# A graph network's edge gathers: more groups fetched by SyncE and ScalarE, and columns prepared one chunk further ahead

## The chip, the cores and the metric

The kernel runs on 1 core of one Trainium2 chip. The metric is the device time of one execution, in microseconds. The engines are TensorE (PE; PEld is its weight load), VectorE (DVE), ScalarE (ACT), GpSimd (POOL) and SyncE (SP, which only issues DMAs).

## The reference, cut to what matters

There are 12500 nodes with 96 features and 200000 edges (src, dst), sorted by dst. Four passes over the edges, called rounds 0 to 3 here, follow each other: two mean aggregations and two maxima.

```python
h = relu(layernorm(x))
n1 = segment_sum(h[src], dst) / max(deg, 1)          # round 0
n2 = segment_sum(n1[src], dst) / max(deg, 1)         # round 1
x = x + 0.5 * n1 + 0.5 * n2
h = relu(layernorm(x))
def egnn(X, Wm, We, Wr, b):                          # rounds 2 and 3
    msg = X[src] @ Wm + edge_attr @ We               # edge_attr: 200000 x 32
    agg = segment_max(msg, dst)                      # 0 where a node has no edge
    return agg + X @ Wr + b
out = x + leaky_relu(egnn(leaky_relu(egnn(h, ...1)), ...2))
```

## The kernel before

**Tables and groups.** Each round gathers rows of 96 floats from a table in HBM (`tables[r]`): h, n1, h @ Wm of round 2, and the same of round 3. The edges are cut into batches of 128, one edge a partition, 4 batches (GRP) make a group, and there are 391 groups. The row numbers lie in `src_sb`. A group is gathered by 4 indirect DMAs of GpSimd (line 412), 128 rows each, into one of RING = 8 slots of `rows`; 8 groups are a sweep, and there are 49 sweeps, the last with 7 groups. The place of a group in its sweep is its seat, and its slot has the same number. GpSimd's program is written out, one gather after the other. Before it fills a slot again it waits until TensorE has used the group 8 before (`picked` in rounds 0 and 1, `rows_ps` in rounds 2 and 3).

**Groups aside.** Some groups aren't gathered by GpSimd. In every 12th sweep (SPAN) the group in seat 3 (SEAT) is fetched by SyncE into a buffer of its own, `side`: 99, 195, 291 and 387. For each of 128 partitions SyncE loads 4 row numbers into registers (`numbers`, line 269) and issues 4 DMAs of one row (line 317): 512 DMAs a group. In rounds 0 and 1 (`side_sums`) it does so in one piece, as soon as TensorE has used the group aside before. In rounds 2 and 3 (`load_units`) SyncE also loads, for each unit of 4 groups, flags (768 KB, line 334) and edge features (256 KB, line 336) into one of two buffers, once the unit before the last one that is loaded has been scanned; the rows aside are spread behind the 24 units of a stretch, 5 or 6 partitions behind each.

**What is done with a group.** Rounds 0 and 1: VectorE makes one-hot matrices of a group two ahead (line 824, and in round 0 also line 829 for counting), TensorE multiplies the rows with them (line 614), and VectorE adds the windows to `comp`, the compressed sums by node (`fold`, line 841). In round 0 ScalarE also writes the node number beside each row (`stage_ids`, line 474), up to 8 groups ahead. Rounds 2 and 3: TensorE adds edge features times weights (line 633) and the transposed rows (line 635) in PSUM, VectorE runs a segmented maximum (line 856), TensorE transposes it back (line 646) and picks each segment's end with one-hots (line 657), and ScalarE copies PSUM into `runT` (line 482) and into `comp` (line 491).

**Between the rounds**, and behind the last, the nodes are worked off in 14 chunks of 7 tiles (`nodes` on each engine). For a chunk ScalarE loads 7 starting columns (`windows_of`, line 269), copies 7 blocks of `comp` into `win_f`, which has two buffers (line 531), TensorE transposes them into one place of PSUM (line 695), ScalarE copies that out into `win_c` (line 551), VectorE and GpSimd make one-hots (lines 929 and 426; POOL_HOTS says how many of 7 are GpSimd's), and TensorE spreads the rows to their nodes (line 719). In rounds 0 and 3 this last step comes one chunk later; in rounds 1 and 2 it comes in the same chunk and in the same PSUM as the transposes, so that the next transposes wait until VectorE has read it (line 987 or 995). ScalarE prepares chunk k + 1 right behind chunk k's copy out. The results go to the next table (line 311) or to the output (line 371).

Of the kernel before, what the change touches and what calls it, by code (L numbers as in the profile page):

```python
# [35 lines left out]
P = 128  # L36
# [10 lines left out]
SPAN = 12  # L47
SEAT = 3
# [3 lines left out]
SIDES = (SWEEPS - 1) // SPAN  # L52
SIDE = [((b + 1) * SPAN) * RING + SEAT for b in range(SIDES)]
UNITS = 2 * SPAN
# [17 lines left out]
assert SIDES * SPAN == SWEEPS - 1 and SEAT < UNIT and SIDE[-1] < GROUPS  # L72
# [33 lines left out]
def gnn(nc, x, srcs, cur, prev, nxt, cur_r, prev_r, eat, wm1, we1, wr1, b1, wm2, we2, wr2, b2, out):  # L106
    with ExitStack() as ctx:
# [36 lines left out]
        side = sb("side", [P, GRP, X])  # L144
# [65 lines left out]
        POOL_HOTS = {0: 2, 1: 7, 2: 5, 3: 4}  # L210
# [13 lines left out]
        side_in = {r: [sem(f"side_rows_landed_{r}_half{k}") for k in range(2)] for r in rounds}  # L224
# [33 lines left out]
        def sweeps(engine, body):  # L258

            body(0, RING, 0, False)  # L260
            for b in range(SIDES):
                at = (b + 1) * SPAN
                with engine.Fori(at - SPAN + 1, at) as i:
                    body(i, RING, b, False)
                body(at, RING if at < SWEEPS - 1 else LAST, b, True)

# [10 lines left out]
        def _(sp):  # L277
# [35 lines left out]
            def side_rows(r, b, p):  # L313

                at = bass.ds(b * (SPAN * RING * GRP) + SIDE[0] * GRP, GRP)
                for k, row in enumerate(numbers(sp.engine, src_sb[p:p + 1, at], N - 1)):
                    sp.dma_start(side[p:p + 1, k, 0:D], tables[r][bass.ds(row, 1), :]).then_inc(side_in[r][k % 2], 16)  # L317

            def side_sums(r):

                for s in range(2):
                    sp.wait_ge(tstored[r][s], 16 * (CHUNKS // 2))
                with sp.Fori(0, SIDES) as b:
                    sp.wait_ge(picked[r], b * (SPAN * RING) + (SEAT + 1))
                    for p in range(P):
                        side_rows(r, b, p)

            def load_units(r):
# [12 lines left out]
                for u in range(2):  # L341
                    unit(0, u, UNIT)

                def stretch(b, last):

                    sp.wait_ge(rows_ps[r], b * (SPAN * RING) + (SEAT + 1))
                    for t in range(UNITS):
                        unit(b * SPAN + (1 + t // 2), t % 2, LAST - UNIT if t == UNITS - 1 and last else UNIT)
                        for p in range(t * P // UNITS, (t + 1) * P // UNITS):
                            side_rows(r, b, p)  # L350

                with sp.Fori(0, SIDES - 1) as b:
                    stretch(b, False)
                stretch(SIDES - 1, True)

            side_sums(0)
# [6 lines left out]
            side_sums(1)  # L363
# [17 lines left out]
        def _(pool):  # L381
# [19 lines left out]
            for r in range(ROUNDS):  # L401
# [31 lines left out]
        def _(act):  # L433
# [32 lines left out]
            for r in range(ROUNDS):  # L466

                def stage_ids(i, n, b, aside):
                    for j in range(n):
                        g = i * RING + j  # L470
                        if after(i, 1):
                            act.wait_ge(picked[0], g - (RING - 1))
                        to = side if aside and j == SEAT else rows[:, j]
                        act.copy(to[:, :, D + 1], node1[:, bass.ds(i * (RING * GRP) + j * GRP, GRP)]  # L474
                                 ).then_inc(ids_ready, 1)

# [47 lines left out]
                def windows_of(k, s):  # L524

                    w = X if r == 0 else D
                    starts = numbers(act.engine, node_base[0:1, bass.ds(k * CHUNK, CHUNK)])
# [51 lines left out]
        def _(pe):  # L579
# [10 lines left out]
            for r in range(ROUNDS):  # L590
                def gathered(i, j, b, aside):

                    if aside and j == SEAT:
                        for k in range(2):
                            pe.wait_ge(side_in[r][k], (b + 1) * (P * GRP * 8))
                        return side
                    seen = i - b if j == SEAT else i
# [73 lines left out]
                if r in sums:  # L671
                    pe.wait_ge(prep, PREP_ALL)
                    sweeps(pe, sum_windows)
                else:
                    if r == 2:
                        pe.wait_ge(s_w, 16 * 8)
                    sweeps(pe, max_windows)
# [70 lines left out]
        def _(dve):  # L748
# [64 lines left out]
            step(dve.memset(side[:, :, D], 1.0))  # L813
            assert steps[0] == PREP_ALL

            for r in range(ROUNDS):
# [61 lines left out]
                if r in sums:  # L878
                    hots(0, 0)
                    hots(1, 1)  # L880
# [21 lines left out]
                sweeps(dve, add_windows if r in sums else run_maxima)  # L902
# [134 lines left out]
```

## Time and profile before

| | us |
|---|---|
| median of 3 runs | 8210.22 (8205.53 to 8218.09) |
| the profiled execution | 8212.45 |
| its span | 8210.7 |
| GpSimd busy | 6032.1 (73%) |
| TensorE busy, weight loads | 5197.4, 3879.2 |
| VectorE, ScalarE busy | 3292.4, 1509.8 |
| mean granted TensorE clock | 0.67 of full |

The span is the time from the first to the last instruction. Busy times overlap each other. "issue" in the chain is time in which an engine waited for nothing that the profile shows. The granted clock has two levels here, 0.5 (1.2 GHz) and 1.0 (2.4 GHz).

### The profile page before, as it was taken

What the parts mean: (1) busy time and instruction counts of PE and PEld (TensorE: products, weight loads), DVE (VectorE), ACT (ScalarE), POOL (GpSimd) and SP (SyncE); (2) the same over time, 40 slices, a digit from 0 to 9 for tenths busy, and PEclk for the clock granted to TensorE, in tenths of its full rate; (3) what the DMA queues carried; (4) which work ended last, traced back from release to release, by engine and by line L of the source; (5) the groups of instructions that cost most, each with busy time, mean ns of one, the idle gap of its engine ahead of it and who ended that gap; (6) DMA issues with size and microseconds to landing.
All of it is one profiled execution on the core that took longest, in us unless ns stands there. A gap on an engine that the chain in (4) does not pass through costs nothing.

```text
span 8210.7 us, 127758 instructions
## 1 busy us (share of the span) xinstructions
PE 5197.4 (63%) x25651; PEld 3879.2 (47%) x25651; DVE 3292.4 (40%) x6694; ACT 1509.8 (18%) x5077; POOL 6032.1 (73%) x6461
## 2 busy tenths in 40 slices
PE   3444444445444444444578888888887887878887
PEld 2333333334333333333556655566565555655556
DVE  5444444444433333333433333333343333333334
ACT  2000000001000000000333333323332332333333
POOL 6777777776677777777667777777766777777776
PEclk6555555555555555555687888878888888888887
DMA  3111111111211111111144444444424444444442
GB/s 91 40 40 40 40 41 40 40 40 41 58 40 40 40 40 41 40 41 40 37 96 91 95 93 92 96 91 92 96 61 96 91 97 91 94 94 91 96 92 70
DMA packets 324280, 551.26 MB, mean 67 GB/s; under 512 B 198824, under 2 KB 198824, under 8 KB 299048
## 3 DMA queue, kind: packets, MB, share of 16 engines
q0 software_dynamic: 198144, 304.75, 18.2%
q1 hardware_dynamic: 125188, 242.68, 11.7%
q14 instruction: 353, 2.89, 0.1%
q8 instruction: 47, 0.77, 0.0%
q10 hardware_dynamic: 548, 0.17, 0.0%
HBM read 522.27 MB, written 24.87 MB: 67 GB/s over the span
## 4 chain that ended last, share of the span: by engine, by line
POOL 65%; issue 22%; PE 8%; DMA 3%; ACT 1%; ACTq 1%; DVE 0%; SPq 0%; DVEq 0%; POOLq 0%
POOL rows L412 65%; DMA rows<-table,src_sb 3%; PE ps L635 2%; PE ps L633 2%; PE ps L657 1%; PE ps L719 1%; PE ps L695 1%; ACTq L269 0%; PE ps L646 0%; ACT arena L457 0%; PE ps L732 0%; ACT arena L531 0%; DMA table<-arena 0%; ACT arena L551 0%; SPq L317 0%
## 5 line engine op out<-in xcount | busy, mean ns | idle before, releaser
L412 POOL DMA_INDIRECT rows<-table,src_sb x6192 | 5848.0, 944 | 1975.8 <-issue 1868.0
L614 PE MATMUL ps<-arena,rows 128*98 128x128 f32 (+1 forms) x6192 | 1557.4, 433 | 2154.0 <-DMA rows<-table,src_sb 1286.8
L614 PEld LDWEIGHTS ps<-arena,rows 128*98 128x98 f32 (+1 forms) x6192 | 1296.4, 279 | 2439.4 <-DVE comp L841 2157.6
L856 DVE TENSOR_TENSOR_SCAN arena<-arena,ps 96x512 f32<-96x512 f32 x782 | 997.6, 1276 | 2450.7 <-PE ps L635 2447.9
L841 DVE TENSOR_TENSOR comp<-comp,ps 98x128 f32 (+1 forms) x3128 | 895.7, 286 | 2262.6 <-PE ps L614 1947.4
L633 PE MATMUL ps<-arena,we 32*96 32x512 f32 x1564 | 1033.6, 745 | 721.5 <-DMA rows<-table,src_sb 704.0
L635 PEld LDWEIGHTS ps<-ident,rows 128*96 128x96 f32 x6192 | 865.9, 195 | 754.1 <-issue 754.1
L824 DVE TENSOR_TENSOR arena<-ps,meta 128x512 f32<-128x512 f32 x1564 | 1050.9, 672 | 32.4 <-issue 28.8
L635 PE MATMUL ps<-ident,rows 128*96 128x128 f32 x6192 | 1062.8, 326 | 0.0
L491 ACT COPY comp<-ps 96x128 f32 x3128 | 818.9, 262 | 1088.4 <-PE ps L657 830.5
L657 PE MATMUL ps<-arena 128*96 128x128 f32 x6256 | 968.5, 306 | 1.6 <-ACT arena L482 1.6
L657 PEld LDWEIGHTS ps<-arena 128*96 128x96 f32 x6256 | 865.2, 193 | 2.1 <-ACT arena L482 2.1
L482 ACT COPY arena<-ps 128x384 f32<-128x384 f32 x782 | 373.8, 478 | 1622.7 <-PE ps L646 1620.8
L633 PEld LDWEIGHTS ps<-arena,we 32*96 32x96 f32 x1564 | 218.4, 182 | 865.4 <-DMA rows<-table,src_sb 708.6
L646 PE MATMUL ps<-ident,arena 96*128 96x96 f32 x3128 | 470.4, 282 | 0.3 <-DVE arena L856 0.3
L646 PEld LDWEIGHTS ps<-ident,arena 96*128 96x128 f32 x3128 | 406.6, 168 | 0.8 <-DVE arena L856 0.8
L474 ACT COPY rows<-root 128x4 f32 (+1 forms) x387 | 75.7, 197 | 1799.0 <-PE ps L614 1799.0
L539 ACT COPY rel_c<-node_rel 128x7 f32<-128x7 f32 (+1 forms) x42 | 8.5, 202 | 1943.0 <-DVE comp L841 1943.0
L426 POOL TENSOR_SCALAR arena<-iota,rel_c 128x128 f32<-128x128 f32 x252 | 170.9, 693 | 191.8 <-ACT rel_c L539 107.5
L829 DVE TENSOR_TENSOR arena<-ps,meta 128x392 bf16<-128x392 f32 x391 | 217.4, 556 | 0.0
L620 PE MATMUL ps<-arena,ones_b 128*1 128x392 bf16 x391 | 189.4, 485 | 0.0
L719 PE MATMUL ps<-arena 128*128 128x96 f32 (+1 forms) x784 | 137.7, 348 | 6.2 <-ACT arena L551 4.8
(91 smaller groups left out, 1068.8 us busy)
## 6 DMA issues: line engine op xcount, KB each, us to landing
arena<-flags SPq DMA_DIRECT2D x194, 768.0 KB
side<-table SPq DMA_DIRECT2D x8192, 0.4 KB
rows<-table,src_sb POOLq DMA_INDIRECT x6192, 2.5
arena<-in_eat SPq DMA_DIRECT2D x194, 256.0 KB
table<-arena SPq DMA_DIRECT2D x56, 336.0 KB, 2.7
out<-xs SPq DMA_DIRECT2D x13, 336.0 KB
xs<-in_x SPq DMA_DIRECT2D x6, 672.0 KB, 5.3
arena<-flags SPq DMA_DIRECT2D x2, 576.0 KB
```

Of the source, the lines that this page charges most:

```text
L412: pool.indirect_dma_start(rows[:, g % RING, j, 0:D], None, tables[r][:, :], bass.IndirectOffsetOnAxis(src_sb[:, c:c + 1], 0)).then_inc(lan ...
L482: act.copy(runT[:, slot % SCANS].rearrange("p k d -> p (k d)"), ps[:, RUNT + slot % 2 * BANK:RUNT + slot % 2 * BANK + GRP * D]).then_inc(r ...
L491: act.copy(comp[0:D, bass.ds(at, P)], ps[0:D, WIN + slot % 2 * BANK + j * P:WIN + slot % 2 * BANK + (j + 1) * P]).then_inc(folded[r], 1)
L614: m = pe.matmul(ps[0:w, at + k * P:at + (k + 1) * P], got[:, k, 0:w], hot[:, j % HOTS, k, :], start=True, stop=True)
L633: pe.matmul(ps[0:D, at:at + W], we[D:P, r - 2, :], fe[D:P, u, q * W:(q + 1) * W], start=True, stop=False)
L635: m = pe.matmul(ps[0:D, at + k * P:at + (k + 1) * P], got[:, k, 0:D], ident[:, :], start=False, stop=(k == GRP - 1))
L646: m = pe.transpose(ps[:, at:at + D], run[:, slot % SCANS, k * P:(k + 1) * P], ident[0:D, 0:D])
L657: m = pe.matmul(ps[0:D, at:at + P], runT[:, slot % SCANS, k, :], hot[:, slot % HOTS, k, :], start=True, stop=True)
L719: m = pe.matmul(ps[:, at_spread + j * P:at_spread + j * P + w], spread_c[:, qs, j, :], win_c[:, qs, j, 0:w], start=True, stop=True)
L824: dve.tensor_tensor(hot[:, slot % HOTS], ids.unsqueeze(1).to_broadcast([P, GRP, P]), rel, ALU.is_equal).then_inc(hot_ready[r], 1)
L841: dve.tensor_tensor(win, win, ps[0:w, of:of + P], ALU.add).then_inc(folded[r], 1)
L856: dve.tensor_tensor_scan(run[:, slot % SCANS], fe[0:D, slot // UNIT, q * W:(q + 1) * W], ps[0:D, ROWS + slot % 2 * BANK:ROWS + slot % 2 * ...
```

## The change

- Which groups are aside now depends on the round. Rounds 0 and 1: every 8th sweep, seats 2 and 3, 6 times two groups, SyncE fetching seat 2 and ScalarE seat 3. Rounds 2 and 3: every 9th sweep, seat 0, 5 groups, by SyncE.
- `side` has two buffers, with semaphores for each.
- The node numbers beside the rows in round 0 are written by VectorE, two groups ahead, and not by ScalarE.
- Between the rounds ScalarE copies chunk k + 2 into `win_f` behind chunk k's copy out, where it was chunk k + 1. Chunks 0 and 1 are done at the start; the registers of chunk 0 are loaded ahead of the wait for the last fold.
- In round 0 GpSimd makes 3 of a chunk's 7 one-hots, where it was 2.

```diff
-SPAN = 12
-SEAT = 3
+SPAN = {0: 8, 1: 8, 2: 9, 3: 9}
+SEATS = {0: (2, 3), 1: (2, 3), 2: (0,), 3: (0,)}
-SIDES = (SWEEPS - 1) // SPAN
-SIDE = [((b + 1) * SPAN) * RING + SEAT for b in range(SIDES)]
-UNITS = 2 * SPAN
+SIDES = {r: (SWEEPS - 1) // SPAN[r] for r in SPAN}
+ASIDE = {r: [(b + 1) * SPAN[r] * RING + seat for b in range(SIDES[r]) for seat in SEATS[r]] for r in SPAN}
...
-        POOL_HOTS = {0: 2, 1: 7, 2: 5, 3: 4}
+        POOL_HOTS = {0: 3, 1: 7, 2: 5, 3: 4}
...
+        def side_rows(engine, r, e, b, p):
+
+            at = bass.ds(b * (SPAN[r] * RING * GRP) + (SPAN[r] * RING + SEATS[r][e]) * GRP, GRP)
+            for k, row in enumerate(numbers(engine.engine, src_sb[p:p + 1, at], N - 1)):
+                engine.dma_start(side[p:p + 1, e, k, 0:D], tables[r][bass.ds(row, 1), :]).then_inc(side_in[r, e][k % 2], 16)
+
+        def side_sums(engine, r, e):
+
+            for s in range(2):
+                engine.wait_ge(tstored[r][s], 16 * (CHUNKS // 2))
+            with engine.Fori(0, SIDES[r]) as b:
+                engine.wait_ge(picked[r], b * (SPAN[r] * RING) + (SEATS[r][e] + 1))
+                for p in range(P):
+                    side_rows(engine, r, e, b, p)
...
-                def stretch(b, last):
-
-                    sp.wait_ge(rows_ps[r], b * (SPAN * RING) + (SEAT + 1))
-                    for t in range(UNITS):
-                        unit(b * SPAN + (1 + t // 2), t % 2, LAST - UNIT if t == UNITS - 1 and last else UNIT)
-                        for p in range(t * P // UNITS, (t + 1) * P // UNITS):
-                            side_rows(r, b, p)
...
+                units = 2 * SPAN[r]
+                with sp.Fori(0, SIDES[r]) as b:
+                    sp.wait_ge(rows_ps[r], b * (SPAN[r] * RING) + (SEATS[r][0] + 1))
+                    for t in range(units):
+                        unit(b * SPAN[r] + (1 + t // 2), t % 2, UNIT)
+                        for p in range(t * P // units, (t + 1) * P // units):
+                            side_rows(sp, r, 0, b, p)
+                with sp.Fori(SIDES[r] * SPAN[r] + 1, SWEEPS - 1) as i:
+                    for u in range(2):
+                        unit(i, u, UNIT)
+                unit(SWEEPS - 1, 0, UNIT)
+                unit(SWEEPS - 1, 1, LAST - UNIT)
...
-                    if g in SIDE:
+                    if g in ASIDE[r]:
                         continue
                     if g >= RING:
-                        pool.wait_ge(used, (g - RING if g - RING not in SIDE else g - 2 * RING) + 1)
+                        pool.wait_ge(used, (g - RING if g - RING not in ASIDE[r] else g - 2 * RING) + 1)
...
-                if r == 0:
-                    sweeps(act, stage_ids)
-                elif r in maxima:
-                    sweeps(act, extract)
+                if r in sums:
+                    act.wait_ge(s_src, 16)
+                    side_sums(act, r, 1)
+                else:
+                    sweeps(act, r, extract)
...
-                act.wait_ge(folded[r], COLS)
...
                         if r:
                             stage_rel(0, 0)
-                        windows_of(0, 0)
+                        first = starts_of(0)
+                        act.wait_ge(folded[r], COLS)
+                        windows_of(0, 0, first)
+                        windows_of(1, 1, starts_of(1))
...
-                        windows_of(k + 1, 1 - s)
+                    if not known(k) or k + 2 < CHUNKS:
+                        windows_of(k + 2, s, starts_of(k + 2))
...
+                def stage_ids(g, j, aside):
+
+                    if after(g, RING):
+                        dve.wait_ge(picked[0], g - (RING - 1))
+                    to = side[:, SEATS[0].index(j)] if aside and j in SEATS[0] else rows[:, j]
+                    dve.tensor_copy(to[:, :, D + 1], node1[:, bass.ds(g * GRP, GRP)]).then_inc(ids_ready, 1)
...
                             hots(g + 2, j + 2)
+                            if r == 0:
+                                stage_ids(g + 2, (j + 2) % RING, aside)
```

The helpers `sweeps` and `gathered` take the round and follow SPAN and SEATS of it.

## Rows read from the trace of the kernel before

**Rows 1.** The page: busy time of each engine; the chain that ended last.

```profile
PE 5197.4 (63%) x25651; PEld 3879.2 (47%) x25651; DVE 3292.4 (40%) x6694; ACT 1509.8 (18%) x5077; POOL 6032.1 (73%) x6461
...
POOL 65%; issue 22%; PE 8%; DMA 3%; ACT 1%; ACTq 1%; DVE 0%; SPq 0%; DVEq 0%; POOLq 0%
```

**Rows 2.** Who waited for what: total us, times, longest.

```profile
POOL rows L412 <- issue: 1868.0, 6127, 0.3
...
POOL rows L412 <- PE ps L635: 18.3, 60, 0.3
...
PE ps L633 <- DMA side<-table: 9.8, 4, 4.8
```

**Rows 3.** Line 412, rounds 0 and 2: ns min/median/max, first and last start.

```profile
L412 POOL DMA_INDIRECT rows<-table,src_sb x1548: 940/944/1936, 60.3 to 1995.8; - x194
...
L412 POOL DMA_INDIRECT rows<-table,src_sb x1548: 940/944/1031, 4134.3 to 6065.7; - x194
```

**Rows 4.** SyncE's timeline, first block of rows aside: start, us.

```profile
89.02 293.89 SPq L317 DMA_DIRECT2D side<-table  x512
```

**Rows 5.** Line 438, ScalarE's one-row DMAs at the start: ns min/median/max.

```profile
L438 ACTq DMA_DIRECT2D wcat<-in_b x2: 321/452/583, 2.3 to 4.5; - x2
```

**Rows 6.** Lines 317 and 269, DMA issues and register loads: count, ns min/median/max.

```profile
L317 SPq DMA_DIRECT2D side<-table x8192: 224/227/321, 89.0 to 8109.9; - x200
...
L269 SPq TENSOR_LOAD <-src_sb x2048: 458/471/745, 88.3 to 8107.9; - x187
...
L269 ACTq TENSOR_LOAD <-base x782: 304/309/327, 4160.4 to 8129.8; - x196
```

**Rows 7.** Windows, GpSimd's gathers: stretch, us, busy (count), clock, DMA share.

```profile
90.00:380.00 290.00, 219.25 (x233) 0.50 0.19 41
390.00:560.00 170.00, 128.52 (x137) 0.50 0.19 39
```

**Rows 8.** SyncE's timeline in round 2: a unit's flags, the rows behind it.

```profile
4620.99 0.32 SPq L334 DMA_DIRECT2D arena<-flags  x1
...
4622.56 13.31 SPq L317 DMA_DIRECT2D side<-table  x24
```

**Rows 9.** TensorE's timeline in round 2, two groups one behind the other.

```profile
4630.01 2.02 PE L633 MATMUL ps<-arena,we 32*96 32x512 f32 x2 [6.01 <-DMA rows<-table,src_sb]
...
4636.26 2.02 PE L633 MATMUL ps<-arena,we 32*96 32x512 f32 x2
```

**Rows 10.** VectorE's timeline at the end of round 2, the last scans.

```profile
6076.82 1.27 DVE L856 TENSOR_TENSOR_SCAN arena<-arena,ps 96x512 f32<-96x512 f32 x1 [1.36 <-PE ps L635]
...
6080.10 1.28 DVE L856 TENSOR_TENSOR_SCAN arena<-arena,ps 96x512 f32<-96x512 f32 x1 [1.42 <-PE ps L635]
```

**Rows 11.** Line 531 behind round 0; TensorE's timeline there.

```profile
L531 ACT COPY arena<-comp x98: 292/293/299, 2006.4 to 2072.5; 98x128 f32 x98
...
2053.21 2.46 PE L719 MATMUL ps<-arena 128*128 128x98 f32 x14
2057.42 1.40 PE L695 MATMUL ps<-ident,arena 98*128 98x98 f32 x7 [1.75 <-ACT arena L531]
2058.62 3.19 PE L719 MATMUL ps<-arena 128*128 128x98 f32 x14
```

**Rows 12.** The timeline behind round 1, TensorE's transposes of the second chunk.

```profile
4032.93 1.36 PE L695 MATMUL ps<-ident,arena 96*128 96x96 f32 x7 [1.04 <-DVE arena L987]
```

**Rows 13.** The page: line 474, ids beside the rows.

```profile
L474 ACT COPY rows<-root 128x4 f32 (+1 forms) x387 | 75.7, 197 | 1799.0 <-PE ps L614 1799.0
```

**Rows 14.** Timelines of round 0: gathers and VectorE's work beside them.

```profile
78.78 1.83 POOL L412 DMA_INDIRECT rows<-table,src_sb  x1 [0.30 <-issue]
...
79.52 0.98 DVE L887 CAST meta<-root 128x1564 bf16<-128x1564 f32 x1
...
415.37 0.56 DVE L829 TENSOR_TENSOR arena<-ps,meta 128x392 bf16<-128x392 f32 x1
415.48 0.94 POOL L412 DMA_INDIRECT rows<-table,src_sb  x1 [0.31 <-issue]
```

More of the change, by code:

```diff
@@ L71 @@
 assert CHUNK * CHUNKS == TILES and CHUNKS % 2 == 0 and RING == 2 * UNIT and UNIT < LAST < RING
-assert SIDES * SPAN == SWEEPS - 1 and SEAT < UNIT and SIDE[-1] < GROUPS
+assert min(SEATS[0]) >= 2 and all(g < GROUPS for r in ASIDE for g in ASIDE[r])
 assert 6 * COLS <= TILES * D and N < NPAD
@@ L143, in gnn @@
         rows = sb("rows", [P, RING, GRP, X])
-        side = sb("side", [P, GRP, X])
+        side = sb("side", [P, 2, GRP, X])
         arena = sb("arena", [P, ARENA])
@@ L222, in gnn @@
         ranked = sem("ranks_in_psum")
-        side_in = {r: [sem(f"side_rows_landed_{r}_half{k}") for k in range(2)] for r in rounds}
+        side_in = {(r, e): [sem(f"side_rows_landed_{r}_{e}_half{k}") for k in range(2)] for r in rounds for e in range(len(SEATS[r]))}
         landed = {r: [sem(f"rows_landed_{r}_slot{k}") for k in range(RING)] for r in rounds}
@@ L256, in chunk, with sweeps @@
             return buffer[:, bass.ds(q * (CHUNK * D), CHUNK * D)].rearrange("p (t d) -> p t d", t=CHUNK)
-        def sweeps(engine, body):
+        def sweeps(engine, r, body):
             body(0, RING, 0, False)
-            for b in range(SIDES):
-                at = (b + 1) * SPAN
-                with engine.Fori(at - SPAN + 1, at) as i:
+            next_to = 1
+            for b in range(SIDES[r]):
+                at = (b + 1) * SPAN[r]
+                with engine.Fori(next_to, at) as i:
                     body(i, RING, b, False)
                 body(at, RING if at < SWEEPS - 1 else LAST, b, True)
+                next_to = at + 1
+            if next_to < SWEEPS:
+                with engine.Fori(next_to, SWEEPS - 1) as i:
+                    body(i, RING, SIDES[r], False)
+                body(SWEEPS - 1, LAST, SIDES[r], False)
+        def side_rows(engine, r, e, b, p):
[9 more added lines that the diff above has]
+                    side_rows(engine, r, e, b, p)
         def numbers(engine, ap, most=NPAD):
@@ L311, in store_table @@
                         sp.dma_start(table_view(tables[r + 1], i * 2 + s), nout[:, s]).then_inc(tstored[r + 1][s], 16)
[L313 to L325, printed above, removed]
-                        side_rows(r, b, p)
             def load_units(r):
@@ L466, in _ @@
             for r in range(ROUNDS):
[L468 to L475, printed above, removed]
                 def copy_running(g, slot):
@@ L518, in _, with starts_of, windows_of @@
                     windows(GROUPS - 1, LAST - 1)
-                act.wait_ge(folded[r], COLS)
                 if r == 0:
                     act.wait_ge(count_steps, 4)
-                def windows_of(k, s):
+                def starts_of(k):
+                    return numbers(act.engine, node_base[0:1, bass.ds(k * CHUNK, CHUNK)])
+                def windows_of(k, s, starts):
                     w = X if r == 0 else D
-                    starts = numbers(act.engine, node_base[0:1, bass.ds(k * CHUNK, CHUNK)])
                     if after(k, 2):
@@ L591, in gathered @@
                 def gathered(i, j, b, aside):
-                    if aside and j == SEAT:
+                    if aside and j in SEATS[r]:
+                        e = SEATS[r].index(j)
                         for k in range(2):
-                            pe.wait_ge(side_in[r][k], (b + 1) * (P * GRP * 8))
-                        return side
-                    seen = i - b if j == SEAT else i
+                            pe.wait_ge(side_in[r, e][k], (b + 1) * (P * GRP * 8))
+                        return side[:, e]
+                    seen = i - b if j in SEATS[r] else i
                     pe.wait_ge(landed[r][j], seen * (16 * GRP) + 16 * GRP)
@@ L812, in _ @@
             step(dve.memset(rows[:, :, :, D], 1.0))
-            step(dve.memset(side[:, :, D], 1.0))
+            step(dve.memset(side[:, :, :, D], 1.0))
             assert steps[0] == PREP_ALL
@@ L878, in _ @@
                 if r in sums:
-                    hots(0, 0)
-                    hots(1, 1)
+                    for g in range(2):
+                        hots(g, g)
+                        if r == 0:
+                            stage_ids(g, g, False)
                 if r == 0:
```

14 lines of the change are left out of this document (5 added, 9 removed).

## The prediction, made before the changed kernel was run

> **What bounds the kernel now.** I read the engines' shares first, then the chain that ended last, the waits, line 412 by rounds, and then the timelines of SyncE and of PE. GpSimd is the busiest engine, 73%, and the chain lies on its gathers, line 412, for 65% of the span and on "issue" for 22% more [rows 1]. The reader should see that this "issue" is the same thing: 6127 gaps of 0.3 us ahead of gathers [rows 2], so one gather costs 0.944 + 0.30 us. In round 2 the 1548 gathers take 1931.4 us from the first start to the last (4134.3 to 6065.7), 1.2485 us each, and 1935.5 us in round 0 [rows 3]. GpSimd never waited for a buffer for longer than that gap [rows 2]. So a round is as long as GpSimd has gathers, and what PE, DVE and ACT do in it is hidden. Four such rounds make some 7.73 ms; the four stretches between and behind them, where chunks of nodes are worked off, hold the rest.
>
> **Fewer gathers.** Before, 4 groups of a round come from SyncE. After, rounds 0 and 1 have 6 times 2 aside and rounds 2 and 3 have 5 each. GpSimd gathers 379 groups instead of 387 twice and 386 instead of 387 twice: 8 + 8 + 1 + 1 = 18 groups, 72 gathers. 72 x 1.2485 = **89.9 us less**, if the rows fetched aside are there in time.
>
> **Are they, in rounds 0 and 1?** SyncE's 512 rows take 293.9 us [rows 4]. Between the two asides of the same seat GpSimd gathers 62 groups, 62 x 4 x 1.2485 = 309.6 us. To SyncE's 293.9 come, by my estimate, 0.8 us of wake-up, 2 us to land and 2 us of matmuls before the buffer is free, 299 in all: it fits with some 10 us to spare. ACT, for seat 3, issues DMAs in the trace only at the start: 0.58 and 0.32 us for a single row of 96 (line 438) [rows 5]; SyncE's take 0.227, with 0.321 as the longest, and of a register load ACT's is the faster, 309 ns against 471 [rows 6]. Bounds for ACT's 512 rows: with SyncE's 0.227, 293.9 - 128 x 0.162 = 273 us; with 0.32, 48 us more, 321 us. I take 273, since SyncE's own first DMA of a block is slow as well and the next are not; the ones in rows 5 are beside SyncE's loads. If a block is late, the cover is GpSimd's run ahead of PE in 8 slots, by my estimate 30 us once a round.
>
> Does a gather get dearer beside the fetches? In 90 to 380 us, with SyncE fetching, 233 gathers in 290 us, and in 390 to 560 us, without, 137 in 170 [rows 7]: 1.245 and 1.241. Nothing.
>
> The dearer case is SyncE and ACT issuing at once, which no row shows over a stretch. Below: no effect. Above: every issue at SyncE's longest, 0.321, +48 us per block, rival (b); I take no effect, the side of rows 7.
>
> **Rounds 2 and 3.** SyncE also loads flags and edge features, a unit per 4 groups. Now it fetches 5 or 6 partitions' rows behind each unit: 24 rows took 13.31 us, from 1.57 us behind the unit's start [rows 8], so 2.2 us a partition. After, 128 partitions on 18 units are 7.1 each: 15.7 + 1.7 = 17.4 us against 20 us a unit. It fits. But the aside group moves from seat 3 to seat 0. Its last 8 partitions' rows are issued behind unit 17, which waits until the group just before it is scanned: 1.7 + 17.8 = 19.5 us, and some 1.5 to land. PE will stand **21 us at each of 5 aside groups** a round, where before it stood 4.8 us at most [rows 2]. Is that hidden? Call the aside group G and count from the unit's issue. The unit at 4620.99 waited for 96 scanned groups, and (4620.99 - 4134.3) / 4.994 = 97.5: GpSimd is in its 98th gathered group, which at the stop, G being left out, is G+2. It asks for the slot of G+1 again at G+9, 0.5 + 6 groups later: 33 us. PE starts G at 21, its rows are in PSUM at 25, and a group at the slow clock takes 6.25 us [rows 9], so G+1 is through at 31, sooner at the fast clock, where a group takes 3.28 [rows 10]. 2 us of slack: hidden when GpSimd is where it was at 4620.99, and 3 us are lost each time that it is a group ahead. I take **+5 us** over the 10 stops; bounds 0, and 60, 6 us each. Then PE goes at SyncE's pace of 17.4 us a unit and has made up its 20 us in 8 of 18 units.
>
> **The ends of rounds 2 and 3.** The last aside group was 387, three from the end, and PE waited for it [rows 2]: in round 2 it is 14.4 us from the last gather's start, 6065.7 [rows 3], to the start of the last scan [rows 10]. Now the last aside group is 360, and PE follows the last gather. With by my estimate 3.5 us to land and 2.2 to 4 us of matmuls that is some 8: 6 less. In round 3 I expect 2 less by the same reason. **-8 us**, bounds -12 and 0.
>
> **Between the rounds.** In round 0 a chunk takes (2072.5 - 1.2 - 2006.4) / 13 = 5.0 us [rows 11]: ACT's copy out of PSUM, a load of 7 registers, 7 copies, transposes on PE, and again. PE stands 1.75 us for ACT ahead of its transposes [rows 11]. One chunk ahead, that wait goes; late next is PE itself, 1.40 + 3.19 us at the slow clock [rows 11], 4.7 with gaps: 0.3 us of 14 chunks, 4 us. At the fast clock, where the second is 2.46, DVE comes next, by my estimate 4.2 us: 12 us. I take 5 there and 4 in round 3, whose order is the same. Rounds 1 and 2 have lag 0: the transposes wait for DVE's read of the PSUM that both use [rows 12], and I take 0. The first chunk pays: the second chunk's load and copies (2.8 us) come ahead of the first copy out, which waited 1.5 us for the transposes: 4 x 1.3 = +5. Registers loaded ahead of the wait for the last fold give back by my estimate 1.2 x 3 = -4. Sum **-8 us**, bounds -22 and +5.
>
> **The ids of round 0** go from ACT to DVE: 391 copies of 0.2 us [rows 13]. DVE is busy for 40% of the span [rows 1] and has room for them. But the gather at 78.78 took 1.83 us instead of 0.94 and lasted until 0.1 us behind the end of DVE's line 887 [rows 14]. A copy of 0.2 us can cost a gather 0.2 at most, 78 us in all; below, nothing, since in the steady state it comes behind line 829, which ends at 415.93, in the middle of the gather that starts at 415.48 [rows 14], and waits seem to arise at a gather's start and end. I take **+3**. The Trainium skill ("SBUF — State Buffer", "SBUF: two separate sides") has a rule that speaks against this move: an fp32 SBUF-to-SBUF tensor_copy locks GpSimd out of the shared port, so that it can't write descriptors. The gather at 78.78 agrees with it; by that rule each copy that meets a gather delays it, 20 us by my estimate at random phases. POOL_HOTS of 3 moves one small operation a chunk from DVE to GpSimd, which has room between the rounds: 0.
>
> **The sum.** The profiled execution is 8212.45 us, its span 8210.7. -89.9 + 5 - 8 - 8 + 3 = -98: 8114.5. The median of the runs shown is 2.2 us lower: **8112**.
>
> **Rivals.**
> (a) The asides are partly late, or PE's stops reach GpSimd. With ACT at 321 us a block the period is 321 + 5 against 309.6: 98 us behind over 6 blocks, less the first block's head start (some 15) and 30 of run-ahead, 53 a round, 106 in all: 8218. With half of that, or the 55 us more of the stops: 8165. For it: SyncE has but 10 us to spare, a stop 2. Against: each late block is covered once more by the ring.
> (b) SyncE and ACT hold each other up, both at 0.321 us an issue. A block is 342 + 5: 6 x 37.4 - 45 = 179 a round, +358: 8470, slower. The gain is gone from 0.28 us an issue: a block 27 us longer, 6 x 16.3 - 45 = 53 a round, 106. For it: ACT's 0.58 while SyncE's loads went out [rows 5]. The Trainium skill ("DMA: Bandwidth & Descriptors", "Queues, rings and completion order") has it that SyncE's and ACT's queues are not descriptor generators of their own; by that rule the two could hold each other up, and no row here shows two streams of small DMAs at once. Against: those loads are of 128 partitions, these of one row, and GpSimd's gathers, a third issuer, don't change SyncE's 0.227.
> (c) The ids' copies meet the gathers: up to +75, 8130 to 8187.
> (d) Nothing is gained between the rounds, with PE at the slow clock the bound: 8120, inside the forecast's own range.
>
> **Chances.** Forecast, with (d), 8090 to 8135: 0.67. (a) or (c) at 8135 to 8190: 0.16; (a) at 8190 to 8230: 0.05. (b): 0.08. Below 8090, with PE at the fast clock between the rounds: 0.04. The range, 8078 to 8195, leaves out some 0.15. 0.2% is 16 us, about what this kernel's measurement can tell: faster 0.85, same 0.06, slower 0.09.
>
> **What would show it.** 6120 gathers at an unchanged 0.944 + 0.30 us; 1892 us (rounds 0 and 1; 4 more in 0) and 1927 to 1932 (2 and 3) from first to last gather; ACT's block of side rows near 273 us and SyncE's 294 in rounds 0 and 1; matmuls of line 633 (as it is numbered before) waiting some 20 us for side rows, 10 times, and gathers waiting for PE by a few us at most. I am wrong if gathers wait for PE in rounds 0 and 1, or if a DMA issue of ACT or SyncE takes over 0.26 us at the median.

## The result and the profile after

| | before | after |
|---|---|---|
| median, us | 8207.88 (8199.66 to 8218.09, 4 runs) | 8144.3 (8104.83 to 8151.17, 4 runs) |
| ratio | | 0.9909, interval 0.9885 to 0.9932 |
| span of the profiled execution | 8210.7 | 8149.4 |

The change takes 0.9% away: 61.3 us from span to span. The time is inside the predicted range (8078 to 8195), but 32 us above the predicted 8112 and outside the forecast's own 8090 to 8135. The changed kernel's executions lie on two levels, near 8143 to 8156 and near 8105 to 8116; the profiled one is of the upper.

The page of the kernel after, shares and chain, against [rows 1]:

```profile
PE 5029.7 (62%) x25651; PEld 3758.5 (46%) x25651; DVE 3314.4 (41%) x7071; ACT 1432.1 (18%) x4686; POOL 5974.3 (73%) x6403
...
ACTq 38%; POOL 27%; issue 19%; PE 9%; DMA 3%; SPq 2%; DVE 1%; ACT 1%; DVEq 0%; POOLq 0%
POOL rows L417 27%; ACTq L276 27%; ACTq L289 11%; PE ps L639 2%; PE ps L637 2%; DMA rows<-table,src_sb 2%; PE ps L661 2%; SPq L276 1%; PE ps L723 1%; PE ps L650 1%; SPq L289 1%; PE ps L736 1%; ACT arena L462 0%; DMA table<-arena 0%; PE ps L618 0%
```

The reader should see ACTq, which had 1% of the chain and now has 38%: ScalarE's queue, with its one-row DMAs (line 276) and its register loads (line 289). The gathers no longer have the chain to themselves. The waits of the same kernel (total us, times, longest), against [rows 2]:

```profile
POOL rows L417 <- issue: 1850.3, 6060, 1.2
...
PE ps L618 <- DMA side<-table: 237.4, 12, 35.4
PE ps L637 <- DMA side<-table: 212.6, 10, 23.6
```

The gaps ahead of gathers are the old 0.3 us. New are PE's 12 waits for rows aside in rounds 0 and 1 (line 618), the longest 35.4 us, and in rounds 2 and 3 the 10 of line 637 that the prediction expected. Line 417 by rounds (ns min/median/max, first and last start), against [rows 3]:

```profile
L417 POOL DMA_INDIRECT rows<-table,src_sb x1516: 938/944/2074, 60.6 to 1959.9; - x190
L417 POOL DMA_INDIRECT rows<-table,src_sb x1516: 940/944/1991, 2062.8 to 3957.1; - x190
L417 POOL DMA_INDIRECT rows<-table,src_sb x1544: 940/944/1031, 4107.6 to 6034.8; - x193
L417 POOL DMA_INDIRECT rows<-table,src_sb x1544: 940/944/1031, 6147.5 to 8073.9; - x193
```

From first to last gather: 1899.3, 1894.3, 1927.2 and 1926.4 us, where 1935.6, 1932.5, 1931.4 and 1931.4 stood. That is 83.7 us less; only 61.3 reach the end. The timeline at the end of round 0 shows what eats the rest:

```profile
1955.47 30.68 ACTq L276 DMA_DIRECT2D side<-table  x52
...
1959.87 0.94 POOL L417 DMA_INDIRECT rows<-table,src_sb  x1 [0.30 <-issue]
...
1987.34 2.00 PE L618 MATMUL ps<-arena,side 128*98 128x128 f32 x8 [35.41 <-DMA side<-table]
```

GpSimd has done its last gather at 1960.8, and ScalarE goes on with one-row DMAs of group 387 until 1986.2. PE stands still for 35.4 us and has three groups more to do. From the last gather's start to the end of the last fold it is 37.7 us in round 0 and 35.2 in round 1, against 7.80 and 7.65 before: **57.5 us lost**. The same stretch in rounds 2 and 3 fell from 20.7 and 16.5 to 14.0 and 14.8. What lies between those ends and the next round's first gather fell by 27.0 us in all (366.9 to 339.9). -83.7 + 57.5 - 8.4 - 27.0, and 0.3 at the start, is the -61.3.

Why ScalarE is late: its issues and register loads over the kernel, and its last block in round 0 (count, ns min/median/max, first and last start), against SyncE's in [rows 4, 6].

```profile
L276 SPq DMA_DIRECT2D side<-table x11264: 224/225/457, 86.6 to 7953.7; - x198
L276 ACTq DMA_DIRECT2D side<-table x6144: 228/229/557, 88.8 to 3980.8; - x199
...
L289 SPq TENSOR_LOAD <-src_sb x2816: 458/470/683, 85.9 to 7951.8; - x188
L289 ACTq TENSOR_LOAD <-src_sb x1536: 312/516/750, 88.1 to 3978.8; - x192
...
L276 ACTq DMA_DIRECT2D side<-table x512: 228/229/542, 1674.6 to 1985.9; - x171
```

The last row is a block of 311.3 us: above the period of 309.6. Six of them start 88.8, 408.4, 725.4, 1041.6, 1357.9 and 1674.6 us into the span, 316 to 317 apart from the second on, each one as soon as PE has used the one before. That is some 7 us more than the period each time, and it adds up: PE's waits for side rows in round 0 are 4.6, 11.9, 18.9, 25.2, 32.0 and 35.4 us, one for each block. GpSimd, running ahead in its ring of slots, notices once, at the fifth, and what it loses there makes the last step smaller:

```profile
1671.82 2.00 PE L618 MATMUL ps<-arena,side 128*98 128x128 f32 x8 [32.05 <-DMA side<-table]
...
1676.45 0.94 POOL L417 DMA_INDIRECT rows<-table,src_sb  x1 [3.33 <-PE ps L618]
```

The medians hide where the time goes; one partition of the block does not. Lines 289 and 276 on ScalarE, in 120.4 to 121.2, 121.1 to 121.7 and 121.75 to 122.8 us:

```profile
L289 ACTq TENSOR_LOAD <-src_sb x1: 538/538/538, 120.5 to 120.5; - x1
...
L276 ACTq DMA_DIRECT2D side<-table x1: 475/475/475, 121.2 to 121.2; - x1
...
L276 ACTq DMA_DIRECT2D side<-table x3: 234/235/235, 121.8 to 122.6; - x3
```

A load, a first DMA of twice the length, three short ones. Over round 0 the first of four has a median of 0.461 us, the others 0.229; SyncE's are 0.269 and 0.225 us.

### The profile page after: what moved, and what is told of

Its sections match the earlier page's. It is cut to its first block, busy times and chain, and to the rows that moved or that the text cites. A ratio compares the mean times of both kernels' runs of the same rounds, so it can differ in the third digit from the quotient of the medians.

```text
span 8149.4 us, 159623 instructions
## 1 busy us (share of the span) xinstructions
PE 5029.7 (62%) x25651; PEld 3758.5 (46%) x25651; DVE 3314.4 (41%) x7071; ACT 1432.1 (18%) x4686; POOL 5974.3 (73%) x6403
## 3 DMA queue, kind: packets, MB, share of 16 engines
q1 hardware_dynamic: 131332, 243.87, 11.9%
## 4 chain that ended last, share of the span: by engine, by line
ACTq 38%; POOL 27%; issue 19%; PE 9%; DMA 3%; SPq 2%; DVE 1%; ACT 1%; DVEq 0%; POOLq 0%
POOL rows L417 27%; ACTq L276 27%; ACTq L289 11%; PE ps L639 2%; PE ps L637 2%; DMA rows<-table,src_sb 2%; PE ps L661 2%; SPq L276 1%; PE ps L723 1%; PE ps L650 1%; SPq L289 1%; PE ps L736 1%; ACT arena L462 0%; DMA table<-arena 0%; PE ps L618 0%
## 5 line engine op out<-in xcount | busy, mean ns | idle before, releaser
L417 POOL DMA_INDIRECT rows<-table,src_sb x6120 | 5780.6, 945 | 1962.5 <-issue 1850.3
L618 PE MATMUL ps<-arena,rows 128*98 128x128 f32 (+1 forms) x6064 | 1481.7, 423 | 1952.3 <-DMA rows<-table,src_sb 1128.1
L618 PEld LDWEIGHTS ps<-arena,rows 128*98 128x98 f32 (+1 forms) x6064 | 1234.5, 272 | 2220.6 <-DVE comp L845 1917.4
L637 PE MATMUL ps<-arena,we 32*96 32x512 f32 x1564 | 1004.1, 726 | 797.2 <-DMA rows<-table,src_sb 534.9
L639 PEld LDWEIGHTS ps<-ident,rows 128*96 128x96 f32 x6176 | 832.9, 189 | 722.4 <-issue 722.4
L639 PE MATMUL ps<-ident,rows 128*96 128x128 f32 x6176 | 1024.9, 318 | 0.0
L661 PE MATMUL ps<-arena 128*96 128x128 f32 x6256 | 943.9, 301 | 1.3 <-ACT arena L478 1.3
L661 PEld LDWEIGHTS ps<-arena 128*96 128x96 f32 x6256 | 840.0, 188 | 1.7 <-ACT arena L478 1.7
L637 PEld LDWEIGHTS ps<-arena,we 32*96 32x96 f32 x1564 | 212.6, 177 | 936.9 <-DMA rows<-table,src_sb 522.7
L530 ACT COPY arena<-comp 96x128 f32 (+1 forms) x392 | 83.8, 295 | 1971.4 <-issue 1956.6
L618 PE MATMUL ps<-arena,side 128*98 128x128 f32 (+1 forms) x192 | 46.2, 420 | 237.4 <-DMA side<-table 237.4
```

Source lines behind the costliest of these rows:

```text
L417: pool.indirect_dma_start(rows[:, g % RING, j, 0:D], None, tables[r][:, :], bass.IndirectOffsetOnAxis(src_sb[:, c:c + 1], 0)).then_inc(lan ...
L618: m = pe.matmul(ps[0:w, at + k * P:at + (k + 1) * P], got[:, k, 0:w], hot[:, j % HOTS, k, :], start=True, stop=True)
L637: pe.matmul(ps[0:D, at:at + W], we[D:P, r - 2, :], fe[D:P, u, q * W:(q + 1) * W], start=True, stop=False)
L639: m = pe.matmul(ps[0:D, at + k * P:at + (k + 1) * P], got[:, k, 0:D], ident[:, :], start=False, stop=(k == GRP - 1))
L661: m = pe.matmul(ps[0:D, at:at + P], runT[:, slot % SCANS, k, :], hot[:, slot % HOTS, k, :], start=True, stop=True)
```

## The experiments

The runs stand in three sets, each with its own runs of the kernel before, to which its ratios belong: 8213.58 us (median) beside again, windows_only, asides_only and span9; 8207.82 beside act_alone, act_p0, load_ahead and drop_last; 8209.33 beside two_loads, seat3 and two_loads_seat3. "Tail" is the stretch from the last gather's start to the end of the last fold.

**again**: the changed kernel as it is.

> The changed kernel once more, for its spread and as the measure for the others on the same chip. Theory L (late blocks): ScalarE's blocks of 512 rows take 311 to 312 us each, the last fold of rounds 0 and 1 ends 35 to 38 us behind the last gather's start, time 8145 us, some 63 below the kernel before. Rival V: the blocks vary from run to run, which is why one of four runs was 40 us shorter: then the block here may be 300 us or less and the time near 8105.

8148.99 us (8115.1 to 8155.67, 6 runs), ratio 0.9905 [0.9888, 0.9922]; tails 37.4 and 36.6. It repeats.

**windows_only**: the kernel before with the second part of the change alone: the columns of `comp` one chunk further ahead, the registers of chunk 0 ahead of the wait, and GpSimd's third one-hot in round 0. The diff shows the first of these.

```diff
...
-                        windows_of(k + 1, 1 - s)
+                    if not known(k) or k + 2 < CHUNKS:
+                        windows_of(k + 2, s, starts_of(k + 2))
...
```

> The kernel before with the second part of the change alone: columns prepared one chunk further ahead, registers of chunk 0 ahead of the wait, POOL_HOTS of 3. Theory: the 14 chunks behind rounds 0 and 3 take some 46 and 43 us from first to last copy out instead of 64 and 63, those behind rounds 1 and 2 4 and 1 us more; about -30 us, 8178. What the prediction said: -8 us, 8200.

8181.11 us (8178.89 to 8194.08, 5 runs), ratio 0.9962 [0.9949, 0.9975]: 32 us less. The 14 copies out of PSUM behind round 0, first and last start, in the kernel before (line 551) and in this one (line 556):

```profile
L551 ACT COPY arena<-ps x14: 730/731/732, 2009.5 to 2073.7; 128x686 f32<-128x686 f32 x14
```

```profile
L556 ACT COPY arena<-ps x14: 718/730/732, 2011.5 to 2056.5; 128x686 f32<-128x686 f32 x14
```

13 chunks take 45.0 us (46.2 in the changed kernel) where they took 64.2. Behind round 3, where POOL_HOTS is unchanged, it is 41.5 us (43.0) instead of 63.3, so the third one-hot can't be what helps there. Windows of PE over that stage (start:end, us, busy, granted clock, DMA share, GB/s), before, and windows_only:

```profile
2006.00:2072.00 66.00, 47.47 (x259) 0.61 0.21 58
```

```profile
2008.00:2060.00 52.00, 34.72 (x280) 0.90 0.29 81
```

The clock that was granted is 0.90 where it was 0.61. PE's busy time is 12.8 us shorter in the second window, though more of its matmuls lie in it, and its idle time only 1.3 us: most of the gain is matmuls at the faster clock. In the changed kernel the clock is 0.84 over 2000 to 2050 us. Its timeline of PE:

```profile
2018.50 1.80 PE L723 MATMUL ps<-arena 128*128 128x98 f32 x14 [1.00 <-DVE arena L999]
2020.13 0.76 PE L699 MATMUL ps<-ident,arena 98*128 98x98 f32 x7
2021.68 1.80 PE L723 MATMUL ps<-arena 128*128 128x98 f32 x14 [0.80 <-POOL arena L431]
```

The transposes have no bracket behind them, where [rows 11] had 1.75 us for ACT; PE now waits about 1 us ahead of the spreading instead, for one-hots of GpSimd and for VectorE. A chunk follows the other in 3.2 to 4.3 us, 3.6 in the mean. Behind rounds 1 and 2 nothing was gained: the 14 copies span 88.6 us in windows_only where they spanned 87.6, and 76.4 where they spanned 75.3. No run takes the three pieces of this part one by one.

**asides_only**: the changed kernel without its second part (the diff above, the other way round).

> The changed kernel without its second part: between the rounds all as before. Theory L: gathers -84 us, tails of rounds 0 and 1 +57, of 2 and 3 -8: -35 us, 8173. Rival: if the two parts hide or hurt each other, the two runs' gains don't add up to the whole, 63 us.

8140.12 us (8134.81 to 8180.59, 6 runs), ratio 0.9917 [0.99, 0.9933]. Two runs near 8180, the profiled one with them, four near 8138. In the profiled one the span is 8178.8 with tails of 38.2 and 34.0, and the chunks back at 66.3 and 63.0 us. Of executions on the upper level the two parts add, within 3 us: 31.9 us less in span here, 32.1 for the windows, 61.3 for both. The median and the ratio above are of the lower level, and not to be held against that of **again**.

**span9**: rounds 0 and 1 have every 9th sweep, 5 times two groups.

```diff
-SPAN = {0: 8, 1: 8, 2: 9, 3: 9}
+SPAN = {0: 9, 1: 9, 2: 9, 3: 9}
```

> SPAN 9 instead of 8 in rounds 0 and 1: 5 pairs of groups aside instead of 6, 349.6 us from one to the next. Theory L: ScalarE's block (312 + 5 us) is in time, the tails of rounds 0 and 1 fall from 37.7 and 35.2 us back to about 8 (-57 us), 2 more groups gathered a round cost 4 x 5.0 = 20 us: 37 us below the changed kernel, 8107. Rival D: the long tails come from VectorE's added copies or from two adjacent groups aside; they stay above 30 us, and the time is 20 above, 8164.

8112.25 us (8109.46 to 8112.93, 4 runs), ratio 0.9874 [0.986, 0.9889]. Four groups more for GpSimd, 17.4 us more of gathers in the two rounds than in the changed kernel, and yet 37 us faster than **again**: the tails are 7.8 and 7.7. The period, 70 groups or 349.6 us, is longer than the block, and the last group aside, 363, has 27 others behind it. This run moves both at once and doesn't part them.

**act_alone**: SyncE fetches nothing in rounds 0 and 1 (GpSimd gathers seat 2), ScalarE fetches seat 3 as in the changed kernel.

```diff
-SEATS = {0: (2, 3), 1: (2, 3), 2: (0,), 3: (0,)}
+SEATS = {0: (3,), 1: (3,), 2: (0,), 3: (0,)}
-            side_sums(sp, 0, 0)
...
-            side_sums(sp, 1, 0)
...
-                    side_sums(act, r, 1)
+                    side_sums(act, r, 0)
```

> The changed kernel, but in rounds 0 and 1 SyncE fetches nothing aside; seat 3 alone is aside, by ScalarE. Theory C (the two streams hold each other up): without SyncE's stream ScalarE's block falls from 311.5 us to about 273, its first DMA behind a register load from 0.461 to 0.23 us. Theory O (ScalarE's own price): the block stays at 311 to 312 us, the load at 0.5 us and the first DMA at 0.46. Six more groups a round are gathered, 12 x 5.0 = 60 us more.

8145.95 us (8144.69 and 8147.2), ratio 0.9924 [0.9906, 0.9943]. Its first block of ScalarE, most of it:

```profile
L276 ACTq DMA_DIRECT2D side<-table x492: 234/235/476, 94.7 to 395.0; - x164
...
L289 ACTq TENSOR_LOAD <-src_sb x123: 492/512/559, 96.8 to 395.4; - x123
```

The loads are at 0.512 us with SyncE silent, too. The blocks take 309.4 to 309.6 us (the first 312.4) against 311.3 to 315.2: ScalarE pays its own price, and SyncE's stream costs it 2 us of 310. The tails are 8.1 and 7.7 us. That is not the shorter block alone: with seat 2 gathered, 63 groups lie between two blocks, 314.6 us, and the blocks start 314 to 317 us apart; a block of 309.5 and the 4.3 us or so from its end to the next one's start just fit. In the changed kernel, with 309.6, they would not. The time is that of the changed kernel, since the 56 us more of gathers take back what the tails give.

**act_p0**: ScalarE reads all its row numbers from partition 0, so the rows that it fetches are not those of its groups.

```diff
-            for k, row in enumerate(numbers(engine.engine, src_sb[p:p + 1, at], N - 1)):
+            for k, row in enumerate(numbers(engine.engine, src_sb[p:p + 1, at] if (r, e) not in ((0, 1), (1, 1)) else src_sb[0:1, at], N - 1)):
```

> The changed kernel, but ScalarE's register loads all read partition 0 of the row numbers (so the rows of its groups are those of partition 0's numbers). If a load from another partition than 0 is what makes it 0.516 us where the loads of the window starts, from partition 0, take 0.309, the block falls by 128 x 0.2 = 26 us to 285 us. If it is the place in the stream (right behind DMA issues), load and block stay as they are.

8112.82 us (8094.12 and 8131.51), ratio 0.9884 [0.9859, 0.9909]. The loads don't fall to 0.31 us; their median is 0.587, and one instruction of address arithmetic ahead of each, 0.05 us and a gap of 0.03, is gone. So reading partition 0 is not what made the loads of [rows 6] short. The blocks, 310 to 311 us behind the first, are 1.2 to 1.4 us shorter, and the tails are 34.6 and 26.7. In round 1 six blocks, each 1.4 us shorter, take 8.5 us off the tail: a block's lateness counts six times. The median of two runs 37 us apart says no more.

**load_ahead**: ScalarE loads a partition's row numbers ahead of the DMAs of the one before.

```diff
...
+                ahead = numbers(engine.engine, src_sb[0:1, at], N - 1)
+                for p in range(P):
+                    here, ahead = ahead, numbers(engine.engine, src_sb[p + 1:p + 2, at], N - 1) if p + 1 < P else None
+                    for k, row in enumerate(here):
...
```

> The changed kernel, but ScalarE loads a partition's 4 row numbers one partition ahead, before it issues the DMAs of the one before. Order of instructions in the block: load (p+1), DMAs (p). If the 0.461 us of the first DMA is a wait for the load just ahead of it to be done with, it stays, and so does the block, 311 us. If it is a wait for the loaded registers, it goes: -128 x 0.23 = -30 us, 282 us a block, no late group, tails of 8 us, and 57 us less: 8088.

8141.52 us (8138.34 to 8146.02, 5 runs), ratio 0.9919 [0.9906, 0.9933]; blocks of 309.9 to 311.2 us behind the first (314.1), tails of 37.7 and 30.4, and the first DMA behind a load still 0.461 us, though it uses registers that were loaded a partition earlier. So it is not a wait for the loaded values; it is the place behind a load.

**drop_last**: ScalarE's sixth block, group 387, goes back to GpSimd in rounds 0 and 1.

```diff
+BLOCKS = {(r, e): SIDES[r] - (r < 2 and e == 1) for r in SPAN for e in range(len(SEATS[r]))}
...
-            with engine.Fori(0, SIDES[r]) as b:
+            with engine.Fori(0, BLOCKS[r, e]) as b:
...
```

> The changed kernel without ScalarE's last block of rounds 0 and 1: group 387 is gathered. Theory L: lateness ends with group 323, and TensorE makes it up in the 67 groups that follow; tails of about 8 us instead of 37.7 and 35.2 (-57 us), one more group a round +10 us: 47 below the changed kernel, 8097. Rival D: tails above 30 us remain, 8154.

8098.94 us (8097.55 to 8102.5, 4 runs), ratio 0.9868 [0.9853, 0.9883]; tails 8.1 and 7.9. One group more a round for GpSimd costs 5.0 and 3.9 us and gives back 29.6 and 27.3. The five blocks that are left are as late as they were (PE waits 31.8 us for the fifth in round 0), and it no longer shows: 67 groups lie behind it.

**two_loads**: ScalarE loads the numbers of two partitions and then issues their 8 DMAs.

```diff
...
+                for p in range(0, P, 2):
+                    both = [numbers(engine.engine, src_sb[q:q + 1, at], N - 1) for q in (p, p + 1)]
+                    for q, found in zip((p, p + 1), both):
+                        for k, row in enumerate(found):
...
```

> The changed kernel, but ScalarE loads the row numbers of two partitions and then issues their 8 DMAs (rounds 0 and 1). Theory O (ScalarE's block is long because the first DMA behind a register load takes 0.461 us and the load behind DMAs 0.516, against 0.229 and 0.309 elsewhere): every second partition loses both, so a block takes 311.5 - 64 x 0.232 = 297 us, and 284 if the second load also falls to 0.31. It then fits the period of 309.6, its last block starts some 34 us sooner, the tails of rounds 0 and 1 fall from 37 to 8 us, and the time is 8149 - 57 = 8092 us. Rival (the extra 0.23 us belongs to every partition, wherever the load stands): blocks stay at 311, tails at 35, time 8142 to 8150.

**8087.86 us** (8083.81 to 8088.94, 5 runs), ratio **0.9849** [0.9836, 0.9861], the lowest of all. Its lines 297 (loads) and 293 (DMAs) over one pair of partitions, the whole last block, and the gathers of round 0:

```profile
L297 ACTq TENSOR_LOAD <-src_sb x2: 313/412/512, 120.6 to 121.2; - x2
...
L293 ACTq DMA_DIRECT2D side<-table x1: 470/470/470, 121.7 to 121.7; - x1
...
L293 ACTq DMA_DIRECT2D side<-table x7: 234/235/235, 122.3 to 124.6; - x7
...
L293 ACTq DMA_DIRECT2D side<-table x512: 228/229/527, 1643.2 to 1926.2; - x171
...
L425 POOL DMA_INDIRECT rows<-table,src_sb x1516: 940/944/2455, 60.0 to 1957.0; - x190
```

The second load takes 0.313 us, seven of eight DMAs 0.235, and a block 283.0 us instead of 311.3: at the lower end of what theory O gave (284). It ends 31 us ahead of the last gather, and the timeline of PE there shows who is waited for now:

```profile
1957.01 0.94 POOL L425 DMA_INDIRECT rows<-table,src_sb  x1 [0.30 <-issue]
...
1961.06 2.00 PE L626 MATMUL ps<-arena,rows 128*98 128x128 f32 x8 [4.77 <-DMA rows<-table,src_sb]
```

Tails are 8.1 and 7.7, with all 6 blocks kept. The 0.46 us comes once for each change from a load to DMAs, the 0.2 us more of a load once for each change from DMAs to a load; halve the changes and both halve.

**seat3**: in rounds 2 and 3 the group aside stands on seat 3 and not on 0.

```diff
-SEATS = {0: (2, 3), 1: (2, 3), 2: (0,), 3: (0,)}
+SEATS = {0: (2, 3), 1: (2, 3), 2: (3,), 3: (3,)}
```

> The changed kernel, but in rounds 2 and 3 the aside groups are on seat 3 instead of seat 0. Theory S (PE's 10 waits of some 21 us at seat 0 reach GpSimd now and then): first to last gather falls from 1927 to 1930 us to 1924 to 1926 in both rounds, PE waits under 8 us for side rows there, and the time is 2 to 8 us below the changed kernel's 8149. Rival (they are wholly hidden): the rounds stay, time 8149.

8146.34 us (8105.69 to 8153.46, 6 runs), ratio 0.9914 [0.9895, 0.9933]. PE's waits for side rows there, against 212.6 us, 10 times, 23.6 in the changed kernel:

```profile
PE ps L637 <- DMA side<-table: 30.9, 9, 5.6
```

The waits fell by 180 us, and first to last gather is 1927.5 and 1926.4 us where it was 1927.2 and 1926.4. The rival holds for these executions: a wait of 21 us at a group aside is hidden, and the 1924 to 1926 us of theory S did not come. With seat 0 it may show through now and then: **again** had 1929.8 and 1930.3, two_loads 1929.1 and 1929.3, and in each a gather waits some 3 us for PE (2.82 us until 4865.7 in **again**, 3.14 until 6487.8 in two_loads). The two executions with seat 3 have no such wait, too few to call it shown.

**two_loads_seat3**: both.

> Both of the above: seat 3 in rounds 2 and 3 and ScalarE's loads in pairs. With theory O and theory S the gains add: 8092 - 2 to 8 = 8084 to 8090 us, under the 8099 of the kernel without ScalarE's last block. If ScalarE's block stays at 311 us, 8141 to 8149.

8088.35 us (8085.23 to 8094.41, 4 runs), ratio 0.9853 [0.9838, 0.9867]: rounds 2 and 3 at 1927.4 and 1926.6, and tails there of 14.7 and 12.1 against 13.2 and 12.6. That is no gain that can be told from nothing, so two_loads stays the best.

## Why the prediction was right, and where it was not

**Fewer gathers: right.** Forecast -89.9, with +5 for stops. The rounds come out near the forecast: 1899.3 us in round 0 for 1896, 1894.3 in round 1 for 1892, 1927.2 and 1926.4 in rounds 2 and 3 for 1927 to 1932. The step from gather to gather stays 1.249 us. In round 0 one stall of 3 us (4.27 us from the gather at 1672.2 to the next) is all that the late ScalarE cost GpSimd: the ring covered lateness in the middle of a round, and its 30 us were sized about right, since PE's wait had reached 32 us by then.

**ScalarE's block: mis-sized.** The prediction took 273 us, bounds 273 and 321; it measured 311.3 to 315.2. Against 273, each of 128 partitions of round 0's last block pays some 0.21 us more for its load (mean 0.524 us against 0.309) and 0.22 more for its four DMAs (mean 0.288 us a DMA, 0.234 on SyncE), 55 us; 16 come back, since from one instruction to the next ScalarE has 29 to 34 ns in the mean and SyncE 28 to 54. The row of the load (0.309 us, [rows 6]) was taken in rounds 2 and 3, where no DMA issue stands ahead of it. The high ends of [rows 5] were a warning that was argued away: "SyncE's own first DMA of a block is slow as well and the next are not". On ScalarE one in four is.

**The cover: right in the middle, missing at the end. This is the step that put the time 32 us off.** The prediction counted lateness against a head start of 15 us and one run-ahead of GpSimd, 30 us, a round. By the working of its rival (a) a block of 312 us would have cost nothing: 312 + 5 against 309.6 is 44 us over 6 blocks, less than 45. What was measured is 29.9 and 27.6 us a round. The prediction did not ask what stands behind the last group aside: three groups, and no more gathers behind which PE could catch up. So the lateness that PE has there comes out at the end, in both rounds: of its wait of 35.4 us in round 0, 29.9 are lost. That is the sign that it had right for rounds 2 and 3 ("the last aside group is 360", -8 forecast, -8.4 measured) and never asked of rounds 0 and 1, where the last aside group stays 387. The experiments settle it: drop_last and two_loads change only ScalarE's blocks, and their medians are 109 and 121 us below the kernel before beside them, where **again** is 65 below its own: 44 and 57 us more, for 47 and 57 forecast.

**Between the rounds: right sign, more than three times too small.** -8 forecast with -22 as the bound; -27 measured in the changed kernel, and -32 for the whole time of that part alone. The prediction took 0.3 us a chunk at the slow clock as the likeliest in round 0, and 4.2 us a chunk for DVE as the next bound at the fast one. In windows_only the stage behind round 0 ran at a granted clock of 0.90 instead of 0.61 (0.84 in the changed kernel), and a chunk took 3.5 us there (3.6) and 3.2 us (3.3) behind round 3, less than the bound of 4.2. PE's idle time for ACT ahead of its transposes went at the same time; which of the two came first no run separates. Rounds 1 and 2 gave nothing, as forecast.

**SyncE at seat 0: right.** 10 waits of 21 us in the mean, longest 23.6, hidden but for 0 to 4 us a round.

**The ids on DVE: +3 forecast, nothing measured.** A gather's mean is 0.9465 us in round 0, and 0.9463 before. Behind the first 21 gathers of that round, of which some are long in both kernels, 372 ran beside such a copy, for 0.9436 us in the mean, and the other 1123 for 0.9435. The changed kernel's copies into `rows` (count, ns min/median/max):

```profile
L869 DVE COPY rows<-root x379: 157/159/414, 73.3 to 1992.4; 128x4 f32 x168, 128x4 f32<-128x4 f32 x22
```

By the rule of the Trainium skill ("SBUF — State Buffer", "SBUF: two separate sides") the copies would have held gathers up, 20 us in all by the prediction's estimate; for copies as short as these the trace does not agree. The gather that had agreed, 1.83 us at 78.78 [rows 14], stood beside an operation of 0.98 us, and the changed kernel has it too, 1.83 us at 79.2.

**Rivals.** (a), the asides partly late, came true in part: the time lies in the 8135 to 8190 that had 0.16, but not by the road that was written there, a loss of GpSimd's in the middle of the round. (b) is refuted: two streams at once cost 2 us a block. (c) is refuted. (d) is refuted in the good direction. Of the two signs of being wrong, the first was met by its letter, by one gather that waited 3.3 us for PE in round 0, within the few us that the prediction also allowed; the second was not, ScalarE's median issue being 0.229 us. Both looked at a median and at the middle of a round; the cost was in every fourth issue and at the end.

**The sum, with what was measured:** -83.7 (forecast -89.9 + 5 + 3 = -82) - 8.4 (-8) - 27.0 (-8) + 57.5 (0), and 0.3 at the start: -61.3 where -98 was forecast. That the total is 37 us off and not 57 is luck: the tails that were not foreseen were in part made up by 19 us more between the rounds than was forecast. The range held because it had been made wide for rivals (a) and (c), not because this loss was in it.

**What stays open.** Most kernels with the late last block have some executions 37 to 42 us shorter than their others: 1 of 4 and 2 of 6 of the changed one, 4 of 6 of asides_only, 1 of 2 of act_p0, 1 of 6 of seat3, but none of 5 of load_ahead. Those without it (span9, drop_last, act_alone and both with two loads) have none such. Blocks that are shorter in those executions would do it: act_p0 shows that 1.4 us less a block take 8.5 us off a round, so by my estimate some 3 us less in each of 12 blocks would give 40. But no profiled execution is of the lower level, so it isn't shown.

## What to carry to other kernels

When a second engine takes work aside, compare its block, with the time from its end to the next one's start, with the period first: what it is too long by adds up over the blocks. Then ask what is left behind the last block: here the ring hid some 30 us of lateness in the middle of a loop and nothing at the end. Price an issue stream by its own pattern, position by position, and not by medians of the same instruction elsewhere; here one change of order, two loads and then eight DMAs, was worth 57 to 61 us. Where the margin is a few us in 310, give back the last block or shorten the stream before adding more.

## What the runs showed of the hardware

- On ScalarE a one-row DMA takes 0.229 us, but 0.461 when it is the first behind a register load, whatever registers it uses; the load of 4 registers takes 0.516 us behind DMAs (0.587 in act_p0, without the address arithmetic ahead of it) and 0.31 behind another load. On SyncE it is 0.225, 0.269 in round 0 (0.260 in round 1), and 0.470 behind DMAs.
- SyncE and ScalarE issuing 512 one-row DMAs each at once cost ScalarE some 2 us of 310, and SyncE at most 1 of 294. The Trainium skill ("DMA: Bandwidth & Descriptors", "Queues, rings and completion order") has it that their queues aren't descriptor generators of their own; at this rate no run shows them more in each other's way than that.
- The gathers of GpSimd kept 1.249 us from one to the next beside both.
- 391 VectorE copies of 128x4 float32 in SBUF (median 0.159 us) beside the gathers of round 0 did not lengthen them: 0.9436 us for those that met one, 0.9435 for the others.
